# GNN and FFN layers on one NeuronCore: 128-row bias operands, and low halves of block-transposed weight chunks moved from VectorE to GpSimd

## What is computed

```
L0 ffn: gates = top-2 softmax of x @ Wg;  h = gelu(x @ W1[e] + b1[e]);  out += gate[e] * (h @ W2[e] + b2[e])     8 experts, H = 1024
L2 gnn: 4 experts of 2 SAGE layers: relu(aggr(h) @ Wl + bl + h @ Wr)
L2 ffn: 8 leaves of a soft tree:    h = gelu(x @ w1[e] + b1[e]);  out += p[e] * (h @ w2[e] + b2[e])               H = 2048
L3 gnn: attention over edges, a @ Wo, layer norm, relu(x @ W1 + b1) @ W2 + b2, layer norm
L3 ffn: routed: h = silu(x @ w1[e].T);  out += comb[e] * (h @ w2[e].T)     8 experts, top 2, H = 1024
        shared: silu(x @ sg_gate.T) * (x @ sg_up.T) @ sg_down.T
```

## Time and profile before

| | |
|---|---|
| median of 3 runs | 678.96 us (678.28 to 680.28) |
| the profiled execution | 676.72 us, its span 675.0 us, mean granted clock 0.985 |
| PE busy | 628.5 us (93%) |
| DVE busy | 549.9 us (81%) |
| ACT busy | 425.1 us (63%) |
| POOL busy | 15.7 us (2%) |
| loaded from HBM | 167.51 MB, 249 GB/s over the span |

### The profile page before, as it was taken

How to read it: one execution, slowest core, us unless ns; L and a number is a source line. 1 busy time by engine, 2 the same in 40 slices (tenths; PEclk the granted TensorE clock), 3 DMA queues, 4 the chain that set the end, 5 groups by cost and what they waited for, 6 DMA issues and landing times.

```text
span 675.0 us, 9379 instructions
## 1 busy us (share of the span) xinstructions
PE 628.5 (93%) x3108; PEld 488.7 (72%) x3108; DVE 549.9 (81%) x629; ACT 425.1 (63%) x510; POOL 15.7 (2%) x40
## 2 busy tenths in 40 slices
PE   5789999998999999999999999998888799999997
PEld 4466777776687876777777777776766577777776
DVE  6789888884589758888888788787878889999984
ACT  2377777744288659677776776773326566666653
POOL 3000000000000000000000000000010000000000
PEclk9899999999899999999999999999898799999999
DMA  8978899983558757889999989899737689999500
GB/s 256 331 254 290 300 326 309 327 293 95 187 225 317 268 187 263 316 307 332 318 336 316 336 314 332 309 255 214 170 83 189 156 225 254 251 255 251 194 1 17
DMA packets 121232, 168.12 MB, mean 249 GB/s; under 512 B 11259, under 2 KB 49148, under 8 KB 121190
## 3 DMA queue, kind: packets, MB, share of 16 engines
q1 hardware_dynamic: 114868, 165.46, 78.5%
q10 hardware_dynamic: 6338, 2.33, 1.6%
HBM read 167.51 MB, written 0.26 MB: 249 GB/s over the span
## 4 chain that ended last, share of the span: by engine, by line
PE 61%; DVE 23%; ACT 7%; issue 6%; POOL 1%; DMA 1%; DVEq 0%; SPq 0%; ACTq 0%; POOLq 0%
PE pre L715 23%; PE y L715 23%; DVE w_lo L1087 8%; PE tp L727 5%; DVE scratch L1063 4%; DVE w_lo L1071 3%; PE pre L722 3%; PE wt L695 2%; ACT w_hi L472 2%; ACT w_hi L452 1%; DVE hT_lo L1142 1%; DVE st L1019 1%; PE pre L841 1%; DMA ends<-in_edge_weight 1%; POOL rstd L411 1%
## 5 line engine op out<-in xcount | busy, mean ns | idle before, releaser
L1087 DVE TENSOR_TENSOR w_lo<-raw,w_hi 128x2048 fp32r<-128x2048 f32 x115 | 259.0, 2287 | 55.9 <-ACT w_hi L472 55.6
L472 ACT ACTIVATE w_hi<-raw 128x2048 fp32r<-128x2048 f32 x116 | 218.0, 1911 | 9.7 <-issue 9.7
L523 ACT ACTIVATE hT_hi<-tp 128x512 fp32r<-128x512 f32 x66 | 39.4, 598 | 108.1 <-PE tp L727 108.1
L715 PE MATMUL y<-w_hi,hT_hi 128*128 128x512 f32 x280 | 85.8, 418 | 0.0
L715 PE MATMUL pre<-w_hi,x_hi 128*128 128x512 f32 x292 | 80.8, 398 | 3.5 <-ACT x_hi L477 2.8
L715 PE MATMUL y<-w_lo,hT_hi 128*128 128x512 f32 x280 | 80.3, 399 | 0.1
L715 PE MATMUL y<-w_hi,hT_lo 128*128 128x512 f32 x280 | 80.3, 399 | 0.0
L715 PE MATMUL pre<-w_lo,x_hi 128*128 128x512 f32 x292 | 78.9, 391 | 0.5 <-DVE w_lo L1087 0.5
L715 PE MATMUL pre<-w_hi,x_lo 128*128 128x512 f32 x292 | 78.4, 390 | 0.0
L695 PE MATMUL wt<-ident,raw 128*128 128x128 f32 x352 | 56.2, 285 | 14.1 <-DVE w_lo L1071 13.1
L1071 DVE TENSOR_TENSOR w_lo<-wt,w_hi 128x512 fp32r<-128x512 f32 x88 | 59.0, 675 | 12.4 <-ACT w_hi L456 12.2
(11 more groups left out here) (261 smaller groups left out, 625.0 us busy)
## 6 DMA issues: line engine op xcount, KB each, us to landing
raw<-in_L_ffn_w SPq DMA_DIRECT2D x80, 1024.0 KB, 6.9
raw<-in_L_ffn_W SPq DMA_DIRECT2D x32, 1024.0 KB, 7.2
raw<-in_L_ffn_w SPq DMA_DIRECT2D x64, 256.0 KB, 5.2
raw<-in_L_gnn_Wr SPq DMA_DIRECT2D x8, 1024.0 KB, 5.7
raw<-in_L_gnn_Wl SPq DMA_DIRECT2D x8, 1024.0 KB, 7.1
raw<-in_L_gnn_W SPq DMA_DIRECT2D x2, 1024.0 KB, 7.4
raw<-in_L_ffn_sg_gate SPq DMA_DIRECT2D x8, 256.0 KB, 9.9
raw<-in_L_ffn_sg_up SPq DMA_DIRECT2D x2, 1024.0 KB, 13.4
```

Source lines behind the costliest of these rows:

```text
L472: act.activation(w_hi[:, g % SPLIT_SLOTS], raw[:, g % RAW_SLOTS], ACT.Copy).then_inc(w_hi_ready, 4)
L523: act.activation(hT_hi[:, (s - 1) % 2], tp[:].rearrange("p (c n) -> p c n", n=P), ACT.Copy).then_inc(hT_hi_ready, 1)
L715: last = pe.matmul(dst, xs[:, k], ws[:, k], start=start and i == 0, stop=stop and i == len(passes) - 1 and bias is None)
L1087: dve.tensor_tensor(w_lo[:, i], w_blocks if blocked(g) else raw[:, g % RAW_SLOTS], w_hi[:, i].bitcast(F32), ALU.subtract).then_inc(w_lo_re ...
```

## The change

- `bias_hl`, `sel_all` and `sel` get 128 rows. Rows from 16 on are zero: GpSimd clears all of `bias_hl` once, in a new memset at the start, and builds `sel_raw` in all rows of `h`. ACT waits for the memset before its first write of `bias_hl`. The bias matmuls contract over 128 rows, the sums are the same.
- The `w_lo` of the blocked chunks comes from GpSimd, a quarter at a time (`split_block`), with a semaphore of its own, `blocked_lo`. DVE's `split_chunk` returns at once for such a chunk.
- DVE's transpose of quarter q waits for GpSimd's quarter q of the blocked chunk before, since both use `w_blocks`.
- SP waits for the four transposes (`w_blocked`) of the blocked chunk whose slot it fills, no longer for its `w_lo`; for other chunks it waits for their own `w_lo`. `w_lo_ready` now counts the other chunks alone.

```diff
-        bias_hl = sb("bias_hl", [16, BL_COL + D], F32R)
+        bias_hl = sb("bias_hl", [P, BL_COL + D], F32R)
-        sel_all = sb("sel_all", [16, E8, P], F32R)
-        sel = sb("sel", [16, 2, P], F32R)
+        sel_all = sb("sel_all", [P, E8, P], F32R)
+        sel = sb("sel", [P, 2, P], F32R)
...
-        sel_raw = h[0:16, :, :].rearrange("p b n -> p (b n)")
+        sel_raw = h[:].rearrange("p b n -> p (b n)")
...
+        def wait_split(engine, g, quarters=4, it=None):
+            before, per_loop = rounded(g)
+            engine.wait_ge(blocked_lo if blocked(g) else w_lo_ready, at(4 * before + quarters, 4 * per_loop, it))
...
-                    sp.wait_ge(w_lo_ready, at(4 * (g - RAW_SLOTS + 1), 32, it))
+                    if blocked(g - RAW_SLOTS):
+                        before = BLOCKED.index(g - RAW_SLOTS)
+                        sp.wait_ge(w_blocked, at(4 * (before + 1), 4 * LOOP_BLOCKED, it))
+                    else:
+                        wait_split(sp, g - RAW_SLOTS, 4, it)
...
+            pool.memset(bias_hl[:].bitcast(F32), 0.0).then_inc(sm("bias_zero"), 1)
+
+            def split_block(g, it=None):
+
+                for q in range(4):
+                    wait_rounded(pool, g, q + 1, it)
+                    pool.tensor_tensor(w_lo[:, g % SPLIT_SLOTS, q], w_blocks[:, q],
+                                       w_hi[:, g % SPLIT_SLOTS, q].bitcast(F32), ALU.subtract).then_inc(blocked_lo, 1)
             for tag in NORMED[1:]:
                 inv_std(tag)
+                if tag == "l3g_mid":
+                    split_block(BLOCKED[0])
+            for g in BLOCKED[1:2]:
+                split_block(g)
+            with pool.Fori(0, (len(BLOCKED) - 2) // LOOP_BLOCKED) as it:
+                for g in BLOCKED[2:2 + LOOP_BLOCKED]:
+                    split_block(g, it)
...
+            act.wait_ge(sm("bias_zero"), 1)
             act.wait_ge(sm("bias_in"), 64)
...
                 if q == 0:
                     dve.wait_ge(landed[g % RAW_SLOTS], at(arrived(g), 64, it))
-                    if g > BLOCKED[0]:
-                        before = BLOCKED[BLOCKED.index(g) - 1]
-                        dve.wait_ge(w_lo_ready, at(4 * (before + 1), 32, it))
+                if g > BLOCKED[0]:
+                    wait_split(dve, BLOCKED[BLOCKED.index(g) - 1], q + 1, it)
...
-                if g >= CHUNKS:
+                if g >= CHUNKS or blocked(g):
                     return
...
             transpose_blocks(G_L3F)
-            split_chunk(G_L3F)
             dve.wait_ge(chunk_done, G_L3G + 4)
```

More of the change, by code:

```diff
@@ L244, in gnn_ffn_kernel @@
         w_lo_ready = sm("w_lo_ready")
+        blocked_lo = sm("blocked_lo")
         w_blocked = sm("w_blocked")
@@ L547, in halve_bias @@
             def halve_bias(cols, raw_cols):
-                act.activation(bias_hl[:, cols], scratch[0:16, raw_cols], ACT.Copy).then_inc(sm("bias_hi"), 1)
+                act.activation(bias_hl[0:16, cols], scratch[0:16, raw_cols], ACT.Copy).then_inc(sm("bias_hi"), 1)
                 act.activation(scratch[0:16, raw_cols], scratch[0:16, raw_cols], ACT.Copy,
@@ L689, in turn_weights @@
                 if q >= 2:
-                    pe.wait_ge(w_lo_ready, at(4 * g + q - 1, 32, it))
+                    wait_split(pe, g, q - 1, it)
                 elif TURNED.index(g) > 0:
-                    before = TURNED[TURNED.index(g) - 1]
-                    pe.wait_ge(w_lo_ready, at(4 * before + q + 3, 32, it))
+                    wait_split(pe, TURNED[TURNED.index(g) - 1], q + 3, it)
                 for c in range(KC):
@@ L711, in product @@
                     if i == KC:
-                        pe.wait_ge(w_lo_ready, at(4 * (g + 1), 32, it))
+                        wait_split(pe, g, 4, it)
                     if i == 2 * KC and low is not None:
@@ L1086, in split_chunk @@
                     wait_rounded(dve, g, 4, it)
-                    dve.tensor_tensor(w_lo[:, i], w_blocks if blocked(g) else raw[:, g % RAW_SLOTS],
-                                      w_hi[:, i].bitcast(F32), ALU.subtract).then_inc(w_lo_ready, 4)
+                    dve.tensor_tensor(w_lo[:, i], raw[:, g % RAW_SLOTS], w_hi[:, i].bitcast(F32),
+                                      ALU.subtract).then_inc(w_lo_ready, 4)
             def top(values, E, k, src, dst):
@@ L1244, in halve_bias @@
             def halve_bias(cols, raw_cols):
-                hl = bias_hl[:, cols]
+                hl = bias_hl[0:16, cols]
                 return dve.scalar_tensor_tensor(out=hl, in0=hl.bitcast(F32), scalar=half[:, 1:2],
```

## The result

| | before, run again beside it | after |
|---|---|---|
| median | 679.42 us (678.28 to 680.28, 4 runs) | 658.75 us (657.70 to 659.56, 4 runs) |
| ratio, 95% interval | | 0.9717 (0.9685 to 0.9749) |
| profiled execution, its span | 676.72, 675.0 us | 658.17, 656.4 us |
| mean granted clock | 0.985 | 0.986 |

A forecast was written before the change was run, and what follows sets the result against it. PE's pace was taken to bound l0f and l2f, a full DVE the last layer. 16.8 + 2.4 + 0.5 + 0.7 - 2.2 = 18.2 us off the median of 678.96 gave 660.8 us, range 652 to 670.

The forecast's parts named there:

- Bias matmuls: In l0f, l2f and l2g, 128 rows instead of 16 save 0.35 us per bias matmul: 16.8 us in sum.
- The last layer's steps: In l3f's steady steps, DVE without its subtraction no longer bounds; 12 steps gain 0.2 us each, 2.4 us (0 to 6).
- GpSimd's quarters: In the last layer, each quarter's subtraction on GpSimd takes 1.1 us (0.57 to 1.7), hidden unless over 2.0 us.
- Slots: In the last layer, SP's finer release of slots gains nothing (0 to 1 us).
- l3g: Norm chain begins 1.6 us sooner, but GpSimd's first quarter holds DVE 1.1 us: net 0.5 us gained.
- First step of l3f: In step 0, the turned quarter's `w_lo` is no longer held by the subtraction and a transpose: 0.7 us saved.
- Memset: At the start, GpSimd's clearing of `bias_hl` holds DVE's one-hot rows: 2.2 us lost (0 to 2.4).
- rows that don't matter: Rival: bias matmuls stay at 0.57 us whatever their row count, kernel at 677.6 us; chance 0.08.
- the exclusion in the steady steps: Rival: GpSimd and DVE exclude each other in the last layer, steps of 10.4 us, kernel at 688 us; chance 0.05.
- PE's bare pace: Rival: in the last layer PE's 0.3 us wait goes too, 3.6 us more gained, 657.2 us; chance 0.15.

The follow-up runs named there:

- the first experiment: Kernel before the change with only the 128-row bias operands, the memset and ACT's wait for it: 664.14 us against 677.71, ratio 0.9792.
- the third experiment: Changed kernel with 64 rows instead of 128 in the bias operands: 677.02 us, ratio 0.999 to the kernel before.

## Why the prediction was right

The forecast was 660.8 us, 18.2 below the median before, and the mechanisms of its two main terms are those it named. That the sum fits the spans as closely as 18.2 and 18.6 is in part luck: the bias matmuls gave 1.2 us less than forecast, the steps of the last layer 0.3 and its first steps 0.9 less, and the clock in l3g and an early edge list in this one profile gave back 1.5 and 1.1. Point by point:

- **Bias matmuls** (forecast 16.8). Shown: 13.6 us net of the memset alone, so 15.8 with its 2.2; 15.6 by stretches. The step shrank by 0.32 to 0.34 us, not 0.35 (the forecast's own 0.57 less 0.227 is 0.343, rounded up there), which is 0.8 us over 40 steps, and the first steps of l0f and l2f gave next to nothing of their 1.4 us (both layers together 13.1 us, 40 x 0.33 = 13.2); l2g gave 2.5 instead of 1.4. That the row count is the cause is shown by the first and the third experiment; how, "PE doesn't load these weights ahead", is read in the rows of the weight loads. The rule of the Trainium skill that was weighed against it ("TensorE: Matmul & The Clock Gate", LDWEIGHTS: the load's time comes from the columns) holds as far as it goes, 0.18 against 0.19 us; that section says nothing on when the load may start, and that was the price. The same page, in "Part 2: What happens when you issue a matmul", says that loads are pulled ahead where the row groups don't conflict or where the load goes to the background buffer. No run here shows which condition 64 rows fail.
- **The last layer's steps** (forecast 2.4; 8.05 to 8.1 us). Measured 8.12 in both parities, mean before 8.287: 12 steps give 2.06. The forecast's 0.40 for a long step was 4.13 less 3.73 us, from quarter 1 to the next `pre` product; that stretch is now 3.80 (580.52 less 576.72). Its 8.51 and 8.07 us were distances of DVE's subtractions. On PE, from `pre` product to `pre` product, steps of 8.46 and 8.12 us alternated before, so the long one lost 0.34 and the short one nothing. What bounds them is the wait for `wt`, by two runs: moving `h` to another place among ACT's quarters took 0.19 and then 0.39 us off every step.
- **GpSimd's quarters** (1.1, bounds 0.57 and 1.7): 1.31, and hidden as said; with 0.62 us more still hidden, with 1.05 more not. The forecast's threshold of 2.0 us lies between the two.
- **Slots**: nothing, as said.
- **l3g** (0.5). The norm's chain began 1.6 us sooner, GpSimd's quarter took 0.93 of it, and from the last product to the transposes it is 5.89 us where it was 6.57, a gain of 0.7; by whole stretches at the same clock it is 0.45. Not foreseen: PE's own transposes of the identity would have hidden the rest even without GpSimd. Both had to go for PE to win 1 us. The other 1.3 to 1.5 us of that stretch are the clock.
- **First step of l3f** (0.7). PE's second `pre` product came 0.57 us sooner by the trace, but the steps behind it, with the routers' work and a stretch at a lower clock, gave 0.8 back. So no gain is seen from this term, and no run tested it alone.
- **Memset** (-2.2). DVE was held for 2.3 us, and the early memset wins 0.4%. Between the two first profiles half of it is hidden by the edge list that came 0.57 us sooner; runs in which it came as before lost 1.6 and 2.4 us.

Of the rivals, rows that don't matter fell with the first experiment; the exclusion in the steady steps with DVE's transposes at 0.70 us beside GpSimd; PE's bare pace didn't come by itself, but was reached when ACT's order was changed. The Trainium skill, "SBUF — State Buffer", "SBUF: two separate sides", says that a VectorE operation in a two-port mode, or one with two SBUF inputs against a GpSimd operation that reads SBUF, shares one pair of ports with GpSimd, and that whichever starts first has it for its whole length. The trace agrees: DVE's `h` times `rstd` plus `affine`, with two SBUF inputs, was held by GpSimd's quarter (1.68 us against 0.75), subtractions from PSUM and block transposes weren't (0.69 and 0.70). GpSimd's memset, which reads nothing, held the one-hot rows, DVE operations with one tensor input, for all of its 2.3 us; by that rule they would be in a two-port mode, which no run here shows.

## What to carry to other kernels

When one matmul in a dense stream is narrower in rows than its neighbours, look at where its weight load starts: if it starts with the matmul and not ahead, padding with zero rows to the neighbours' 128 can pay. Here it gave back 0.33 us a matmul and cost one memset of 2.3 us, which was free where DVE stood waiting anyway. Work taken off a full engine is worth only the distance to the next bound (here 0.17 us of 2.29 a step), so find that bound's chain before the change and reorder it too; that was worth twice as much as the move. Where an engine fills a gap on purpose, its filler is part of the path, and a gain that ends before the filler does isn't seen.

## What the runs showed of the hardware

- A bias matmul with 64 rows costs as much as one with 16: 6.50 and 6.48 us a step, 6.14 with 128.
- GpSimd's subtraction of 128x512 takes 1.31 us with two different inputs and an fp32r output, and 1.05 when both inputs and the float32 output are one buffer; 0.62 for 256 columns of that.
- A memset on GpSimd held DVE for its full 2.3 us.
- The granted clock behind the same pause of PE was 0.51 in one run and 1.00 in another of the same code. The slower run had two stretches at half clock in l3g, together worth 2.4 us (42.91 against 40.54).
